# Reordering the opening of a two-layer conditional kernel: all first-layer weights and the mask loaded ahead of x's second half

## The reference

```python
# layer 0: weights mixed per batch out of 8 groups
masked_w = weight * mask[None]                       # 8 x 256 x 256
w_bot = jnp.einsum('bg,got->bot', cond, masked_w)
x = x + jnp.einsum('bnt,bot->bno', x, w_bot) + bias
# layer 1: two of 8 experts chosen by cond, and a shared one
rw = softmax(cond); w, sel = top_k(rw, 2); w = w / w.sum()
x = x + sum_k w_k * mlp(x, expert sel_k) + mlp(x, shared)
# mlp(x) = (gelu(x @ gate) * (x @ up)) @ down, inner width 1024
```

## Time and profile before

| | |
|---|---|
| median of three runs | 411.5 us (411.23 to 411.63) |
| profiled execution, its own time | 411.14 us |
| its span in the trace | 409.1 us |
| TensorE busy | 404.4 us, 99% of the span |
| granted TensorE clock | 1.00 throughout |
| first gate/up matmul of the MLP | 14.56 us after the start of the span |
| DMA moved | 35.21 MB, 86 GB/s on average |

### The profile page before, as it was taken

One profiled execution on the slowest core, in us unless ns is written; L12 is line 12 of the kernel. 1 busy time (PEld: TensorE's weight loads), 2 busy tenths in 40 slices (PEclk: granted clock), 3 DMA queues, 4 the chain that ended last, 5 costly groups with the idle time before them and its releaser, 6 DMA issues.

```text
span 409.1 us, 7375 instructions
## 1 busy us (share of the span) xinstructions
PE 404.4 (99%) x2199; PEld 351.0 (86%) x2199; DVE 301.7 (74%) x518; ACT 254.1 (62%) x483; POOL 313.3 (77%) x322
## 2 busy tenths in 40 slices
PE   8999999999999999999999999999999999999997
PEld 5788888888888888888888888888888888889886
DVE  5788876567769888765777889857687767677784
ACT  4887776666564677664646666757455556666541
POOL 1699999999729689999625969999670977999630
PEclk9999999999999999999999999999999999999999
DMA  8653332323200623323010262223200042241201
GB/s 300 211 149 91 100 121 88 103 79 104 77 2 4 199 56 109 104 101 103 28 26 1 56 198 79 77 77 108 72 26 26 2 144 62 77 136 47 53 1 51
DMA packets 18894, 35.21 MB, mean 86 GB/s; under 512 B 2098, under 2 KB 2610, under 8 KB 18866
## 3 DMA queue, kind: packets, MB, share of 16 engines
q1 hardware_dynamic: 18576, 34.61, 27.5%
q10 hardware_dynamic: 290, 0.26, 0.2%
HBM read 32.77 MB, written 2.10 MB: 85 GB/s over the span
## 4 chain that ended last, share of the span: by engine, by line
PE 97%; DVE 1%; ACT 0%; issue 0%; POOL 0%; DVEq 0%; POOLq 0%
PE o_ps L582 16%; PE g_ps L528 11%; PE u_ps L527 11%; PE u_ps L528 11%; PE u_ps L531 11%; PE g_ps L527 10%; PE g_ps L531 10%; PE p_ps L582 9%; PE l_ps L482 2%; PE p_ps L590 2%; PE p_ps L591 1%; PE u_ps L432 1%; PE o_ps L631 0%; PE p_ps L447 0%; DVE t_raw L1000 0%; DVE out_sb L1157 0%
## 5 line engine op out<-in xcount | busy, mean ns | idle before, releaser
L1268 POOL TENSOR_TENSOR eg_lo<-raw_g,eg_hi 128x512 fp32r<-128x512 f32 x64 | 91.6, 1452 | 10.4 <-ACT eg_hi L747 10.4
L780 ACT ACTIVATE gelu<-g_ps 128x512 f32<-128x512 f32 x95 | 56.9, 599 | 53.2 <-PE g_ps L531 51.8
L1076 DVE SCALAR_TENSOR_TENSOR u_ps<-gelu,route_cur,u_ps 128x512 f32<-128x512 f32 x64 | 48.1, 752 | 50.9 <-PE u_ps L531 47.7
L1112 DVE TENSOR_TENSOR h_both<-t_raw,h_both 128x1024 fp32r<-128x1024 f32 x46 | 76.4, 1661 | 0.5 <-ACT h_both L813 0.5
L1310 POOL TENSOR_TENSOR ed_lo<-s_raw,ed_hi 128x512 fp32r<-128x512 f32 x30 | 51.7, 1722 | 0.0
L800 ACT CAST h_both<-u_ps 128x256 fp32r<-128x256 f32 x46 | 17.2, 373 | 54.8 <-DVE t_raw L1091 33.4
L528 PE MATMUL g_ps<-x_hi,eg_lo 128*128 128x512 f32 (+1 forms) x128 | 50.2, 392 | 0.0
L527 PE MATMUL g_ps<-x_hi,eg_hi 128*128 128x512 f32 (+1 forms) x128 | 50.0, 391 | 0.0
L527 PE MATMUL u_ps<-x_hi,eg_hi 128*128 128x512 f32 (+1 forms) x128 | 49.8, 389 | 0.0
L528 PE MATMUL u_ps<-x_hi,eg_lo 128*128 128x512 f32 (+1 forms) x128 | 49.8, 389 | 0.0
L813 ACT CAST h_both<-t_raw 128x1024 fp32r<-128x1024 f32 x46 | 47.9, 1041 | 0.5 <-DVE t_raw L1098 0.5
(11 more groups left out here) (232 smaller groups left out, 1048.6 us busy)
## 6 DMA issues: line engine op xcount, KB each, us to landing
raw_g<-experts SPq DMA_DIRECT2D x64, 256.0 KB, 2.8
raw_d<-experts SPq DMA_DIRECT2D x32, 256.0 KB, 2.7
raw_g<-shared SPq DMA_DIRECT2D x8, 256.0 KB, 5.5
l_raw<-l_w SPq DMA_DIRECT2D x3, 512.0 KB, 5.6
x_in<-xT SPq DMA_DIRECT2D x6, 256.0 KB, 3.7
outT<-out_sb SPq DMA_DIRECT2D x6, 256.0 KB, 3.0
raw_d<-shared SPq DMA_DIRECT2D x4, 256.0 KB, 2.9
x_in<-xT SPq DMA_DIRECT2D x1, 512.0 KB, 4.3
```

The lines of the kernel that those rows point to most:

```text
L780: act.activation(gelu[:, s % 2], l0_ps if at_first(b) and s == 1 else g_ps, ACT.Gelu_apprx_tanh).then_inc(gelu_done, 1)
L1076: dve.scalar_tensor_tensor(u_ps[:, s % 2], gelu[:, s % 2], route_cur[:, k:k + 1], u_ps[:, s % 2], ALU.mult, ALU.mult).then_inc(h_done, 1)
L1112: dve.tensor_tensor(h_lo[:, at], t_raw[:], h_hi[:, at].bitcast(F32), ALU.subtract).then_inc(t_lo_done, 1)
L1268: pool.tensor_tensor(eg_lo[:, j % RING], raw_g[:, j % RAW_G], eg_hi[:, j % RING].bitcast(F32), ALU.subtract).then_inc(gu_lo_done, 1)
```

## The change

SP loads in another order and brings x in two halves: half 0 weights, all eight groups, the mask, half 0 of x, half 1 weights, all eight groups, and then half 1 of x. `load_x_0` is gone; `load_x_half` is used for batch 0 too, with a semaphore for each half.

Group 6 of half 0 goes from TensorE to VectorE, so that half 0 is mixed by five groups on VectorE and three on TensorE; one `diag` and one `mix_l0` fewer are made. `pass_x(0)`, all of half 1's `mix_l0` and the contraction are interleaved in `first_layer_0`, block by block: the block (output half 0, input half 0) is applied as soon as its weights are there, between the mixes of half 1.

```diff
-        DIAGS = (2, 3, 6, 7, 5)
+        DIAGS = (2, 3, 7, 5)
...
             load_l0(0, 0)
-            load_x_0()
             load_l0(0, 1)
+            sp.dma_start(mask[:], l0_mask).then_inc(mask_in, 16)
+            load_x_half(0, 0)
             load_l0(1, 0)
-            sp.dma_start(mask[:], l0_mask).then_inc(mask_in, 16)
             for i in range(2):
                 load_l0_last(i)
+            load_x_half(0, 1)
             shared_weights()
...
             def first_layer_0():
+                pass_x(0)
+                mix_l0(1, 2, first=True)
                 pe.wait_ge(first_hi_done, 1)
-                for th in range(HH):
-                    first_layer_part(l0_hi, 0, th, x_hi)
+                first_layer_part(l0_hi, 0, 0, x_hi)
+                mix_l0(1, 3)
+                pass_x_rest(0)
+                first_layer_part(l0_hi, 0, 0, x_lo)
+                pe.wait_ge(first_lo_done, 1)
+                first_layer_part(l0_lo, 0, 0, x_hi)
+                mix_l0(1, 5)
                 mix_l0(1, 7, last=True)
-                for th in range(HH):
-                    first_layer_part(l0_hi, 0, th, x_lo)
-                pe.wait_ge(first_lo_done, 1)
-                for th in range(HH):
-                    first_layer_part(l0_lo, 0, th, x_hi, last=(th == HH - 1))
-                for th in range(HH):
-                    pe.wait_ge(first_hi_done, 2 + th)
-                    for x in (x_hi, x_lo):
-                        first_layer_part(l0_hi, 1, th, x)
+                pass_x(1)
+                first_layer_part(l0_hi, 0, 1, x_hi)
+                first_layer_part(l0_lo, 0, 1, x_hi)
+                pe.wait_ge(first_hi_done, 2)
+                first_layer_part(l0_hi, 1, 0, x_hi)
+                pe.wait_ge(x_lo_done, 2)
+                first_layer_part(l0_hi, 0, 1, x_lo, last=True)
+                first_layer_part(l0_hi, 1, 0, x_lo)
+                pass_x_rest(1)
+                pe.wait_ge(first_hi_done, 3)
+                for x in (x_hi, x_lo):
+                    first_layer_part(l0_hi, 1, 1, x)
                 for th in range(HH):
                     pe.wait_ge(first_lo_done, 2 + th)
                     first_layer_part(l0_lo, 1, th, x_hi, last=(th == HH - 1))
...
             mix_l0(0, 2, first=True)
             mix_l0(0, 3)
-            pass_x(0)
-            keep_warm(1)
-            pass_x(1)
-            mix_l0(0, 6)
             mix_l0(0, 7, last=True)
-            for hh in range(HH):
-                pass_x_rest(hh)
-            mix_l0(1, 2, first=True)
-            for g in (3, 5):
-                mix_l0(1, g)
+            keep_warm(2)
             first_layer_0()
```

In `first_gate_up` the four matmuls of a half with high input go in the order gate high, gate low, up high, up low, each behind its own wait, where it was gate high, up high, gate low, up low. On ACT and VectorE:

```diff
-            for hh in range(HH):
-                split_x(0, hh)
+            split_x(0, 0)
+            split_l0_0()
             scale_first()
-            split_l0_0()
             act.activation(gelu[:, 0, 0:8], shifted[:, 0], ACT.Gelu_apprx_tanh)
-            split_gate(0)
+            split_x(0, 1)
             for th in range(HH):
                 split_l0_1(th)
+            split_gate(0)
+            first_x1_hi(0)
             split_up(0)
-            first_x1_hi(0)
...
             route_top()
             route_sums()
-            route_pair()
-            route_weigh()
             combine_0(0, 0)
             combine_0(0, 1)
-            for hh in range(HH):
-                first_x_lo(hh)
+            route_probs()
             combine_0(0, 4)
             combine_0(0, 5)
+            combine_0(0, 6)
             add_mixed_0()
             apply_mask_0()
+            first_x_lo(0)
+            split_l0_0()
             combine_0(1, 1)
             combine_0(1, 4)
-            split_l0_0()
             combine_0(1, 6)
             for th in range(HH):
                 add_mixed_1(th)
                 apply_mask_1(th)
+            first_x_lo(1)
             for th in range(HH):
                 split_l0_1(th)
             for oh in range(HH):
                 first_x1_lo(oh)
+            route_pair()
+            route_weigh()
             route_index()
```

More of the change, by code:

```diff
@@ L282, in load_l0_last @@
                 sp.dma_start(l0_raw[:, 1, at], l0_w[1, 1, :, bass.ds(2 * i * D, 2 * D)].rearrange("p (g d) -> p g d", d=D)).then_inc(l0_in[3 + i], 16)
-            def load_x_0():
-                sp.dma_start(x_in[:], xT[0]).then_inc(x_loaded[0], 16)
             def shared_gu(c):
@@ L508, in first_gate_up @@
                     pe.wait_ge(x1_hi_done, hh + 1)
-                    for ps, off, hi_done in ((g_ps, GATE, part_hi_done), (u_ps[:, 0], UP, gu_hi_done)):
+                    for ps, off, hi_done, lo_done in ((g_ps, GATE, part_hi_done, part_lo_done), (u_ps[:, 0], UP, gu_hi_done, gu_lo_done)):
                         at = off + hh * P
@@ L512, in first_gate_up @@
                         pe.matmul(ps, w_hi[:, at:at + P], x1_at(x1_hi, 0, hh), start=(hh == 0), stop=False)
-                    for ps, off, lo_done in ((g_ps, GATE, part_lo_done), (u_ps[:, 0], UP, gu_lo_done)):
-                        at = off + hh * P
                         pe.wait_ge(lo_done, 1)
@@ L695, in split_x @@
             def split_x(b, hh):
[L696 to L699, removed]
+                act.wait_ge(x_loaded[hh], 16 * b + 16)
                 if hh == 0 and not at_first(b):
@@ L968, in route_sums, with route_probs @@
                 dve.reciprocal(exp_rsum[:], exp_sum[:]).then_inc(weighed, 1)
+            def route_probs():
                 dve.wait_ge(weighed, 2)
@@ L998, in combine_0 @@
                     else:
-                        dve.wait_ge(first_mixed, {1: 1, 4: 2, 5: 3}[g] if oh == 0 else {4: 5, 6: 6}[g])
+                        dve.wait_ge(first_mixed, {1: 1, 4: 2, 5: 3, 6: 4}[g] if oh == 0 else {4: 6, 6: 7}[g])
                     dve.scalar_tensor_tensor(acc, w, cond_all[:, 0, g:g + 1], acc, ALU.mult, ALU.add).then_inc(first_mixed, 1)
             def add_mixed_0():
-                dve.wait_ge(first_mixed, 4)
+                dve.wait_ge(first_mixed, 5)
                 dve.wait_ge(mixed, 1)
@@ L1013, in add_mixed_1 @@
                 at = slice(D + th * P, D + (th + 1) * P)
-                dve.wait_ge(first_mixed, 7)
+                dve.wait_ge(first_mixed, 8)
                 dve.wait_ge(mixed, 2)
```

## The result

The changed kernel is slower: 413.7 us at the median of ten executions (412.6 to 415.77) against 411.44 (410.92 to 412.18) in ten of the kernel before, ratio 1.0066 with a 95% interval of 1.0051 to 1.0081. That is 2.3 us, clear of the scatter. The profiled execution took 413.58, its span is 410.9 where it was 409.1.

A forecast was written before the change was run, and what follows sets the result against it. TensorE, busy 99% of the span, bounds the kernel; only its unbroken stream's start (14.56 us) can move. 411.14 + 0.67 + 0.1 = 411.9 profiled; median 411.5 + 0.75 = 412.25, range 411.0 to 414.0.

The forecast's parts named there:

- the forecast's own range: Range of the steady forecast for the whole kernel: +0.3 to +1.2 us, alone 411.8 to 412.7, chance 0.60.
- the rival in which half 1's mixes run at the low rate: Opening on TensorE: high clock comes late, some 1.4 us more than the forecast, 414 in all; chance 0.13.
- Half 0: Opening: add_mixed_0 at 7.5 instead of 9.29, l0_hi at 8.9 instead of 10.7; 1.8 us gained, not what TensorE waits for last.
- Half 1's mixes: TensorE in the opening: all four come after weights 10 (8.66), end at 11.7; add_mixed_1 starts 0.28 ahead of 12.00.
- `first_x_lo(1)` behind the masks: VectorE, end of the first-layer stage: x's second low part follows add_mixed_1 and the masks, ending at 13.46.
- seven matmuls after it: TensorE before gate/up: seven matmuls remain after x_lo's second piece, so the stream starts at 15.23 against 14.56, +0.67 us.
- POOL's 0.1: Gate/up start: split_up(0) behind first_x1_hi(0) makes POOL's weight late, about 15.85 against 15.7 wanted; +0.1 us, bounds 0 and 0.25.
- the same bytes ahead of each place give ...: Opening loads: landing follows bytes queued ahead; x's half 0 at 7.4, weights 10 at 8.66, x's half 1 at 10.7.
- bounds 0 and 0.2 us; I take 0: Opening loads: price of moving x as two pieces of 256 KB, taken as 0 from 395 GB/s at 10.70 to 13.00.
- The clock: TensorE's opening: matmul rate doubles near 8.4 us after work without a hole from 4.52; work until then taken as equally dense.
- Outside the span: Around the profiled span: 2.0 us kept unchanged in the sum for the profiled execution.
- 0.67 by order: Start of TensorE's unbroken stream: the new order of work delays it from 14.56 to 15.23, +0.67 us.

The follow-up runs named there:

- e11: Changed kernel with mask late, first_x_lo(1) ahead of the masks, split_up(0) earlier, mixes and matmuls reordered, keep_warm(3): 412.05 us, ratio 1.0011 against the kernel before.
- e14: Kernel before with x loaded at its old place in two halves (rows of 2 KB), nothing else: 412.5 us, ratio 1.0026.
- e12: Kernel before without its keep_warm(1) between the two passes of x: 413.11 us, ratio 1.0033.
- e16: Kernel before with one more keep_warm, ahead of mix_l0(0, 6): 411.4 us, ratio 0.9995.
- e7: Changed kernel's computation with the loads of the kernel before (x whole second, mask behind the first half 1 weights): 416.29 us, ratio 1.0118 against the kernel before.
- e15: Changed kernel with weights 10 (groups 0 to 3 of half 1) loaded in front of the mask and x's half 0: 414.28 us, three executions.
- e9: Changed kernel, with SP waiting for weights 10 before it issues the shared gate/up weights: 414.63 us, ratio 1.0064 against the kernel before.
- e5: Changed kernel with the mask loaded early as rows of 1024 bytes, the bias separately behind x's half 1: 414.88 us, ratio 1.0071 against the kernel before.
- e13: Changed kernel with keep_warm(6) for keep_warm(2), and keep_warm(2) between pass_x(0) and half 1's first mix: 412.98 us, ratio 1.0033 against the kernel before.
- e3: Changed kernel with keep_warm(5) for keep_warm(2): 413.07 us, ratio 1.0028 against the kernel before.
- e10: Changed kernel with keep_warm(3) for keep_warm(2), one more filler matmul: 414.36 us, ratio 1.0077 against the kernel before.
- e4: Changed kernel with first_x_lo(1) ahead of add_mixed_1 on VectorE: 413.17 us, ratio 1.0036 against the kernel before.

## Why the prediction was wrong

The forecast was +0.75 us, no measurable change, with 0.40 on slower; measured is +2.3. The order of work was read rightly, and three inputs were not: the landings, the clock as part of the same chain, and the time outside the span. 413.7 lies inside the wide range of 411.0 to 414.0, but that is luck. The upper end of it was the rival in which half 1's mixes run at the low rate, and in the profiled execution (413.58) they ran at the high one (two instructions in 0.67); the forecast's own range ended at 412.7.

*Half 0.* Right: `add_mixed_0` at 7.45 (7.5), `l0_hi` at 8.78 + 0.40 = 9.2 (8.9, held up by x's late half on ACT). As predicted, it bought nothing.

*Half 1's mixes, `first_x_lo(1)` behind the masks, seven matmuls after it, POOL's 0.1.* Right in mechanism and size, as the three differences in the first section and the row of the weight load at 16.85 show. Moving `first_x_lo(1)` took 0.58 out. With the terms removed in e11 the kernel comes to within 0.11% of the one before.

*The landings.* This is the step that failed first: "the same bytes ahead of each place give ..." and "bounds 0 and 0.2 us; I take 0". In the changed kernel weights 10 landed 0.9 behind their 8.66. In seven more traces where the mask and a half of x lie ahead of them (either order), they landed at 9.4 to 10.6, 0.8 to 1.9 behind. With the mask late or x whole under the new computation the lag is smaller (0.2 to 1.0), but e14, with the mask late and only x split, has 1.3. The loads of the kernel before put weights 10 down at 8.66, 9.27, 8.56 and 9.3 (its own trace, e12, e16 and e7), so my table also took one good execution for the rule: up to 0.7 comes without any short row. What the short rows add shows best from 5 to 7 us. In the five traces in which only rows of 4 KB travel there the queue moves 344 to 397 GB/s (e7, e12, e15, e16 and the kernel before), in the thirteen others 195 to 328. That x's split alone costs 0.9 us is shown by e14.

The row that I took the price from, 395 GB/s from 10.70 to 13.00, was of a later time, and of short rows among short rows. Late short rows run at the full rate in the changed kernel too (389 to 414 GB/s from 10 to 13 us). Whether it is the time, before about 8 us, or the long rows beside them that makes short rows slow stays open: e15's landings speak for the time, its row at 7.00 to 8.00 for the rows. Why the queue moves less there, with the DMA engines partly idle (busy share 0.82 in the changed kernel, 0.75 in e9) and partly at work (0.97 in e14), is not settled either. The odd length of the mask's rows (e5) and SP's issues (e9) are not needed for it.

The fixed 2 us of a transfer that the Trainium skill gives for GpSimd's path ("DMA: Bandwidth & Descriptors", section "Anatomy of one DMA — SWDGE (gpsimd) path"), read as a queue, would have put x's half 1 at 12.7; it landed at 11.6. These transfers are issued by SP, and the trace shows no such 2 us between queued ones: x's half 1 landed 0.7 behind the last quarter, and all of its lag of 0.9 was there already when weights 10 landed. That the estimate pointed to a later landing was luck.

*The clock.* The rival was there, with 0.13, "against: the work up to 8.4 is as dense as before". The reasoning stopped at the rise; what matters too is that the clock falls again, which e5's stretch at 0.50 after the hole shows. Three of ten executions of the changed kernel have a clock of 0.995 or 0.996, as e5's and e9's profiled executions have, with spans 1.7 to 2.5 us over 410.8; none of the twelve of e13 does. These three weren't profiled, so that the fall in them is inferred from the mean. e12 shows the other side, a rise that comes late: one filler less and 0.33%. In e13 the slow spans are gone and the mean span is 0.3 us shorter; as far as these means show it, that is what the hole costs through the clock, on average. The hole of 1.15 us before 9.02 came mostly from the landings: x's half 0 at 8.26 and not 7.4, and at 8.0 to 9.3 in the seven others. So the two are one chain, and my treating them as independent was the second error. The Trainium skill ("TensorE: Matmul & The Clock Gate", section "What's actually happening") says that the gate opens on activity and closes after idleness; e5's trace agrees, with TensorE busy for 0.04 of the 2 us from 8 to 10 and the granted clock at 0.50 in 11.20 to 14.40.

*Outside the span.* The prediction kept 2.0 us outside. It is 2.7 in the changed kernel, 0.6 to 0.7 of the 2.3 us, and 1.8 in e3 and e13, the variants with the most filling. All that those two gain at the median is this time. It isn't one number in any kernel: of 35 executions of the kernel before 13 have 2.4 to 2.9 and the rest about 2.0, of the ten of the changed kernel nine have 2.3 to 3.0, of the twelve of e13 none has more than 2.0. The cause is open, and the number of matmuls on TensorE (e10, e12) doesn't account for it.

The sum for the profiled execution: 0.67 by order, 0.89 by landing and 0.06 of small differences are the 1.62 at the start of the stream; POOL's 0.1 stands behind it, and about 0.1 more isn't assigned, 1.8 in the span (410.9 for 409.1). Outside it are 2.7 for 2.0. Together that is the 2.4 from 411.14 to 413.58. Over ten executions, the three in ten with the lower clock lift the upper half.

## What to carry to other kernels

Where a load is split into shorter rows in the middle of a full queue, don't price it by its bytes or by one trace: look at the landings of several executions, at the time at which it will travel. Fillers on TensorE in an opening are part of the schedule: each wait that a reordering adds there, even 0.5 us, has to be priced with the clock at its low rate over what follows, in the share of executions that it hits (eight of twelve in e12, three of ten in the changed kernel). A half of the work that is ready earlier is worth nothing when the stream starts on the other half. And where a variant is faster, look whether its span is shorter before naming a cause inside it.

## What the runs showed of the hardware

With one matmul of 0.43 us left out of the opening the kernel took 1.5 us more at the median (e12). The instant at which the clock rises differs between executions of nearly the same opening: mixes reach the high rate in the group at 4.24 in e13 (six in 2.40 us) and in none before 12 us in e4. The same loads in the same order put weights 10 down at 9.41 in one kernel's trace (e10) and 10.58 in another's (e3).
